# Cross probabilities of layers 2 and 3: transposed by a DMA in two-byte planes, in place of transposes on TensorE

## The chip, the cores and the metric
The kernel runs on one core of one Trainium2 chip. The metric is the device time of one execution in microseconds (us). One execution in addition was taken with the hardware profiler; all rows below come from it. TensorE is PE in the profile (its weight loads PEld), VectorE is DVE, ScalarE is ACT, GpSimd is POOL, and SyncE, which issues all DMAs here, is SP.

## The reference, cut to what matters
Four transformer layers run one after another on `x` (32 batches, 112 tokens, 256 features). All attend to a context `ctx_1024` (32 batches, 375 tokens, 256 features), with 16 heads.

- Layer 0: RMS norm, cross attention with heads of 64 (four shared heads of keys and values), no feed-forward.
- Layer 1: self attention, cross attention with heads of 16, both with 8-bit fake quantisation of queries, keys, values and probabilities, then a gated feed-forward.
- Layer 2: cross attention with 16 heads of 64, all with own keys and values, then a feed-forward with ReLU.
- Layer 3: causal self attention, cross attention with heads of 16, and a feed-forward with ReLU.

The part that matters is the same in all of them:

```python
scores = einsum('bhtd,bhsd->bhts', Q, K) * D ** -0.5
wei = softmax(scores, axis=-1)                 # 112 tokens x 375 context tokens for each head
o = einsum('bhts,bhsd->bhtd', wei, V)
```

The scores come out with the 112 tokens on partitions. The product with V contracts over the 375 context tokens, so the probabilities have to be transposed between the two.

## The kernel before, in words
Batches go in 16 streams of two. Each layer runs over its 16 streams. Activations lie transposed (features on partitions), so that every projection is a few matmuls of 128 x 128 weights against 224 columns (two batches of 112 tokens). All of it is float32 but for layer 1's quantised values, which are bf16.

**Attention.** An *octet* is eight heads of one batch; a *pair* is two heads, four pairs to a cross octet. A *unit* is one head of a cross pair (a unit of self attention holds four heads). For each pair there are these steps, on these engines:

1. `scores` on PE, into one of four PSUM banks, 112 x 375 each. Layers 0, 2 and 3 (`QUADS`) do the scores of two pairs together; they wait for the exps of the pairs before, which free the banks.
2. `max` on DVE (L1595), the negated maximum of each row.
3. `exp` on ACT (L1460), into `e`, which has ES = 8 slots, four pairs' worth, with the sums.
4. `invert` on DVE (L1602), one over the sums.
5. `weigh` on POOL (L1850), each unit's exps times one over its sum, in place, one instruction for each unit.
6. `turn` on PE (`tensor_turn`, L1287): for each unit three transposes of 112 x 125 against the identity, into one of the four `ring` banks of PSUM, and a save by DVE or ACT (L1675, L1500), a copy of 125 x 336 into `probs`. The slots of `e` come free with it.
7. `pv` on PE (L1322 in layer 2, L1329 in layer 3): the product of values and `probs`, an octet at a time. `probs` has two slots, so an octet waits for the product of two octets before.

Layer 1 doesn't turn on PE. DVE writes its 8-bit probabilities as bf16 into `steps` (`eight`, L1637, four slots), and SP issues one transposing DMA for each pair (`flip`, L1878) straight into `probs`. A cross pair of layer 1 has 2 x 3 blocks of 128 columns. Layer 1 therefore cuts the 375 context tokens into 128, 128 and 119 rows, and the other layers into three times 125 (`R`).

**Order.** Each engine's instruction stream is one fixed list that class `Plan` writes at build time. Every step has a place (its pair's index plus an offset) and an assumed cost in microseconds. `arrange` plays the schedule forward with these costs: an engine that is free takes the ready step with the lowest place, and the list that comes out is what the engine executes in order, with semaphore waits for what each step needs. Steps marked "VA" go to DVE or ACT, whichever is free first. PE may run up to `AHEAD = 6` places ahead. "D" is SP's queue: context loads, stream loads, weights, stores and flips, in one order. The costs assumed for a cross pair are among others 1.15 for `weigh`, 0.35 for the PE part of a turn, 0.5 for its save, and 2.5 for a flip of layer 1. A product `pv` is placed at the index of its octet's last pair plus 2.7 (`TURN_LAG` + 0.5), in layer 1 plus 3.4.

In layer 3 a stream has 16 cross pairs and 4 pairs of self attention of the next stream, so 20 pairs; in layer 2 it has 16.

## Time and profile before

| | us |
|---|---|
| median of 3 runs | 4999.22 (4997.36 to 5001.67) |
| the profiled execution, its own time | 5001.85 |
| its span, first to last instruction | 5000.1 |
| PE busy in the span | 4600.5 (92%) |
| DVE, ACT, POOL busy | 2935.6, 2821.5, 2007.6 |

The profile numbers time from the span's start. Layer 0 runs up to about 940, layer 1 to about 2230, layer 2 to about 3840 and layer 3 to the end, with some overlap. "Busy" is the time in which an engine executes something; the granted clock (PEclk) is a share of TensorE's full 2.4 GHz. "Idle before" names what ended an engine's waits. A float32 matmul is in the records as two.

### The profile page before, as it was taken

To read this page: it belongs to the slowest core of one execution; us is meant where nothing else is said; L and a number is where in the kernel's file an instruction comes from. 1 tells how busy PE (TensorE), PEld (TensorE's weight loads), DVE (VectorE), ACT (ScalarE), POOL (GpSimd) and SP (SyncE) were. 2 spreads that over 40 slices of the span, in tenths; PEclk is the share of its full clock that TensorE was granted. 3 is DMA by queue.
4 is the path that set the end of the run, shared out by engine and by line. 5 is a ranking of instruction groups with operands and counts; after the bars stand their busy time and mean duration, and the time that the engine had idled before them with its cause. 6 is when DMAs were issued, how large, how long until landed. Compare 5 with 4: busy or idle time off the path is not lost.

```text
span 5000.1 us, 86857 instructions
## 1 busy us (share of the span) xinstructions
PE 4600.5 (92%) x32032; PEld 3401.8 (68%) x32032; DVE 2935.6 (59%) x6466; ACT 2821.5 (56%) x8969; POOL 2007.6 (40%) x3876
## 2 busy tenths in 40 slices
PE   8999999876877777789999999999999999999998
PEld 5666666655656556567777777777777777777777
DVE  6566556566656665664544454445445766676665
ACT  4555555688888888863333333333334666666664
POOL 3333333466565665642222222222223444444443
PEclk9999999988889888899999999999999999999999
DMA  2000000133333333331000000000000100000000
GB/s 82 21 24 21 25 23 21 51 67 62 64 62 61 62 67 56 68 69 39 11 14 14 14 11 14 14 14 11 14 23 23 37 15 21 21 18 16 20 17 7
DMA packets 279638, 161.54 MB, mean 32 GB/s; under 512 B 244528, under 2 KB 261168, under 8 KB 277808
## 3 DMA queue, kind: packets, MB, share of 16 engines
q1 hardware_dynamic: 279216, 155.99, 12.9%
q8 instruction: 256, 4.19, 0.4%
q14 instruction: 166, 1.36, 0.1%
HBM read 82.53 MB, written 14.68 MB: 19 GB/s over the span
## 4 chain that ended last, share of the span: by engine, by line
PE 83%; ACT 8%; POOL 3%; DVE 2%; issue 2%; DMA 2%; SPq 0%; ACTq 0%; POOLq 0%; DVEq 0%
PE ring L1340 49%; PE ring L1287 11%; PE score L1273 11%; ACT e L1460 5%; PE ring L1322 3%; PE ring L1315 3%; PE ring L1329 2%; DMA probs<-steps 2%; POOL e L1850 1%; PE ring L1284 1%; POOL e L1847 1%; PE ring L1305 1%; ACT work L1521 1%; PE ring L1355 1%; DVE nmax L1595 1%
## 5 line engine op out<-in xcount | busy, mean ns | idle before, releaser
L1850 POOL TENSOR_SCALAR e<-e,rsum 112x375 f32<-112x375 f32 (+1 forms) x2048 | 1067.4, 540 | 2214.8 <-DVE rsum L1602 2178.9
L1500 ACT COPY probs<-ring 125x336 f32<-125x336 f32 (+1 forms) x971 | 400.1, 448 | 1648.2 <-PE ring L1287 1533.9
L1595 DVE TENSOR_REDUCE nmax<-score 112x2 f32<-112x750 f32 (+1 forms) x1152 | 1064.7, 951 | 420.6 <-PE score L1273 420.5
L1460 ACT ACTIVATE e<-score,nmax 112x375 f32<-112x375 f32 (+1 forms) x2048 | 1039.1, 539 | 42.5 <-DVE nmax L1595 38.2
L1340 PE MATMUL ring<-h,weights 128*128 128x224 f32 x3840 | 876.0, 369 | 30.0 <-ACT work L1521 24.9
L1273 PE MATMUL score<-keys,q 64*112 64x375 f32 (+2 forms) x3584 | 608.4, 494 | 232.4 <-ACT e L1460 229.6
L1340 PEld LDWEIGHTS ring<-h,weights 128*128 128x128 f32 x3840 | 724.9, 197 | 104.4 <-ACT work L1521 33.7
L1287 PEld LDWEIGHTS ring<-consts,e 112*125 112x125 f32 x4608 | 584.5, 188 | 230.8 <-issue 178.9
L1287 PE MATMUL ring<-consts,e 112*125 112x112 f32 x4608 | 645.4, 279 | 4.6 <-POOL e L1850 2.6
L1340 PE MATMUL ring<-weights,ctx 128*125 128x512 f32 (+3 forms) x1536 | 588.4, 516 | 0.0
L1273 PEld LDWEIGHTS score<-keys,q 64*112 64x112 f32 (+2 forms) x3584 | 233.0, 166 | 509.2 <-ACT e L1460 287.1
L1460 ACT ACTIVATE e<-score,nmaxc,quant 112x375 f32<-112x375 f32 (+1 forms) x1024 | 555.1, 553 | 10.7
L1340 PE MATMUL ring<-ctx,weights 128*128 128x375 f32 x1536 | 552.4, 485 | 0.2 <-ACT rdev L1509 0.2
L1847 POOL TENSOR_SCALAR e<-e,rsumw 112x375 f32<-112x375 f32 (+1 forms) x1024 | 497.0, 504 | 30.2
L1460 ACT ACTIVATION_READ_ACCUMULATOR e<-score,nmax 112x1 f32 x2048 | 461.7, 225 | 0.0
L1340 PEld LDWEIGHTS ring<-weights,ctx 128*125 128x125 f32 (+2 forms) x1536 | 305.0, 203 | 142.5 <-issue 95.5
L1340 PE MATMUL ring<-work,weights 128*128 128x224 f32 (+1 forms) x1792 | 398.7, 372 | 1.0 <-DVE work L1718 0.6
L1340 PEld LDWEIGHTS ring<-ctx,weights 128*128 128x128 f32 x1536 | 280.5, 191 | 143.2 <-issue 36.5
L1741 DVE COPY values<-ring 125x512 f32<-125x512 f32 (+2 forms) x419 | 196.7, 495 | 302.6 <-PE ring L1340 301.6
L1675 DVE COPY probs<-ring 125x336 f32<-125x336 f32 (+1 forms) x693 | 335.9, 510 | 41.1 <-PE ring L1287 26.6
L1340 PEld LDWEIGHTS ring<-work,weights 128*128 128x128 f32 x1792 | 334.2, 190 | 32.0 <-issue 5.6
L1340 PE MATMUL ring<-heads,weights 128*128 128x224 f32 x1536 | 323.6, 359 | 3.6 <-ACT work L1521 1.8
(123 smaller groups left out, 5104.9 us busy)
## 6 DMA issues: line engine op xcount, KB each, us to landing
ctx<-ctx_t SPq DMA_DIRECT2D x128, 375.0 KB, 3.1
out_t<-x SPq DMA_DIRECT2D x64, 224.0 KB, 1.9
x<-out_t SPq DMA_DIRECT2D x48, 224.0 KB, 2.6
weights<-weights SPq DMA_DIRECT2D x7, 1024.0 KB, 6.2
probs<-steps SPq DMA_TRANSPOSE x320, 2.7
x<-x_t SPq DMA_DIRECT2D x16, 224.0 KB, 2.6
weights<-weights SPq DMA_DIRECT2D x1, 3328.0 KB, 12.3
weights<-weights SPq DMA_DIRECT2D x1, 2304.0 KB, 9.4
```

Of the source, the lines that this page charges most:

```text
L1273: ins = pe.matmul(score_bank(u)[0:S, n * width:(n + 1) * width], lhs, rhs, start=not masked, stop=not masked or n == nt - 1)
L1287: ins = pe.transpose(dst[0:R, c * S:(c + 1) * S], src[:, c * R:(c + 1) * R], idt[0:S, 0:S])
L1315: ins = pe.matmul(ps[64 * odd:64 * odd + 64, 0:4 * S], vs[0:R, c, kv:kv + 64], probs_of(o, c, 4 * odd, 4 * S), start=c == 0, stop=c == last)
L1322: ins = pe.matmul(ps[64 * odd:64 * odd + 64, i * S:(i + 1) * S], vs[0:R, c, hd:hd + 64], probs_of(o, c, 4 * odd + i, S), start=c == 0, sto ...
L1340: ins = pe.matmul(out_, a, b_, start=n == 0, stop=n == len(parts) - 1)
L1460: ins = nc.scalar.activation(e_of(u)[:, n * width:(n + 1) * width], score_bank(u)[0:S, n * width:(n + 1) * width], ACT.Exp, bias=minus, sc ...
L1500: ins = nc.scalar.copy(dst, src)
L1595: ins = dve.tensor_reduce(to, src, AX, ALU.max, negate=True)
L1675: ins = dve.tensor_copy(dst, src)
L1741: ins = dve.tensor_copy(dst, src)
L1847: ins = nc.gpsimd.tensor_scalar(mine, mine, rsumw[0:S, slot(u), n:n + 1], ROUND, ALU.mult, ALU.add)
L1850: ins = nc.gpsimd.tensor_scalar(mine, mine, rsum[0:S, slot(u), n:n + 1], 0.0, ALU.mult, ALU.add)
```

## The change
It concerns the cross attention of layers 2 and 3 (`WORDS`). Step 6 is replaced, the rest stays:

- `split` (POOL): the two-byte halves of the weighed float32 probabilities of a pair are taken apart into two planes in `halves` (three slots): one `tensor_scalar` (times 1, plus 0) on uint16 for each plane, 112 x 750 elements with a stride of two. It frees the slots of `e`.
- `flip` (SP): one transposing DMA for each pair, 112 x 1536 two-byte elements (2 planes x 2 heads x 3 blocks of 128), into `planes` (two slots). It waits for the split and for the merge of two pairs before.
- `merge` (DVE or ACT): one copy for each pair puts the two planes together again as float32 in `probs`, 128 x 1344 two-byte elements.
- The chunks of the context in layers 2 and 3 go from 125, 125, 125 rows to 128, 128, 119.
- `pv` waits for the merges, and is placed at the last pair's index plus 3.9 in layer 2 and 4.3 in layer 3; the last projection of layer 3's cross attention, its norm and the feed-forward are placed 0.7 later.
- `steps` of layer 1 shares the memory of `halves`.

```diff
+WORDS = (2, 3)
+SPLIT_BY = ("G",)
+SPLITS = 3
+PLANES = 2
@@ place_attention
-                if o.layer != 1:
+                if o.layer != 1 and not self.in_words(o):
                     self.turn_of[u] = self.job(p.index + lag + 0.1 * i, "turn", o.layer, o.s, o.b, 0, "VA", u)
...
-                self.pv_of[o] = self.job(p.index + (3.4 if o.layer == 1 else lag + 0.5), "pv", o.layer, o.s, o.b, o.half, PV_BY[o.layer], o)
+                self.pv_of[o] = self.job(p.index + (3.4 if o.layer == 1 else (4.5, 0, 3.9, 4.3)[o.layer] if self.in_words(o) else lag + 0.5), "pv", o.layer, o.s, o.b, o.half, PV_BY[o.layer], o)
+    def in_words(self, o):
+        return o.layer in WORDS and o.attn == "cross"
@@ narrow
+        e += 0.7 if layer == 3 else 0
@@ list_steps
+            if self.in_words(o_):
+                by = SPLIT_BY[self.nth_halved[p] % len(SPLIT_BY)]
+                self.add("split", p, by, 1.7, p.index + 1.4)
+                self.add("flip", p, "D", 4.2, p.index + 1.6)
+                self.add("merge", p, "VA", 1.45, p.index + 2.4)
@@ four_layers
-        steps = sb("steps", [P, STEPSLOTS, 8 * P], BF16)
+        halves = sb("halves", [P, SPLITS, 4 * CHUNKS * P], U16)
+        steps = halves[:, :, :].rearrange("p a n -> p (a n)")[:, 0:STEPSLOTS * 8 * P].bitcast(BF16).rearrange(
+            "p (a n) -> p a n", a=STEPSLOTS)
+        planes = sb("planes", [P, PLANES, 4 * CHUNKS * S], U16)
...
+        def split(eng, wait, p):
+            wait.wait_ge(weighed, nth["weigh", p])
+            for before in plan.halves_before(p):
+                flip_done(wait, before)
+            to = halves_of(p).rearrange("p (h a n) -> p h a n", h=2, a=2)
+            src = e[0:S, pair_slots(p), 0:T].bitcast(U16).rearrange("p a (n h) -> p h a n", h=2)
+            return [(to[:, h, :, 0:T], src[:, h, :, :]) for h in range(2)]
+
+        def merge(wait, p):
+            flip_done(wait, p)
+            wait.done([plan.pv_of[o] for o in plan.probs_before(p.octet)])
+            to = merged_of(p).rearrange("p a n -> p (a n)").bitcast(U16).rearrange("p (m h) -> p m h", h=2)
+            return to, planes_of(p).rearrange("p (h m) -> p m h", h=2)
@@ chunk
-            return (P * c, min(T, P * c + P)) if layer == 1 else (R * c, R * c + R)
+            return (P * c, min(T, P * c + P)) if layer == 1 or layer in WORDS else (R * c, R * c + R)
@@ scalar_program, vector_program
+                    to, src = merge(wait, x_)
+                    nc.scalar.copy(to, src).then_inc(merged["A"], 1)
...
+                    dve.tensor_copy(to, src).then_inc(merged["V"], 1)
@@ scalar_exp
+                elif plan.in_words(before.octet):
+                    wait.wait_ge(halved[plan.split_by[before]], nth["split", before])
@@ pool_program
-            nc.gpsimd.memset(steps[:, :, :], 0.0).then_inc(consts_made, 1)
+            nc.gpsimd.memset(halves[:, :, :], 0).then_inc(consts_made, 1)
+                if kind == "split":
+                    for to, src in split(pool, wait, x_):
+                        ins = nc.gpsimd.tensor_scalar(to, src, 1.0, 0.0, ALU.mult, ALU.add)
+                    ins.then_inc(halved["G"], 1)
+                    continue
@@ sync_program
+                    if plan.in_words(p.octet):
+                        wait.wait_ge(halved[plan.split_by[p]], nth["split", p])
+                        i = plan.nth_halved[p]
+                        if i >= PLANES:
+                            before = plan.halved[i - PLANES]
+                            wait.wait_ge(merged[plan.by[before]], nth["merge", before])
+                        sp.dma_start(planes_of(p).rearrange("p (a n) -> p a n", n=S), halves_of(p),
+                                     transpose=True).then_inc(turned[n % FLIPS], 16)
+                        continue
```

## Rows read from the trace of the kernel before

**Rows 1.** The page's head: span, and each engine's busy time
```profile
span 5000.1 us, 86857 instructions
...
PE 4600.5 (92%) x32032; PEld 3401.8 (68%) x32032; DVE 2935.6 (59%) x6466; ACT 2821.5 (56%) x8969; POOL 2007.6 (40%) x3876
```

**Rows 2.** Busy time by stretch: one stream of layer 2, four of layer 3
```profile
core 0: us, PE busy (x) PEld busy (x) DVE busy (x) ACT busy (x) POOL busy (x), PEclk, DMA share, GB/s
2427.53:2527.80 100.27, 100.27 (x601) 70.95 (x601) 49.08 (x99) 33.52 (x101) 21.12 (x36) 1.00 0.05 13
...
4242.12:4385.11 142.99, 137.22 (x1369) 112.05 (x1369) 98.70 (x239) 90.64 (x339) 66.25 (x140) 0.98 0.07 19
4385.11:4527.90 142.79, 136.64 (x1374) 111.15 (x1373) 99.43 (x241) 91.22 (x343) 66.25 (x140) 0.99 0.06 19
```

**Rows 3.** The chain of waits by line, first stretches of layers 2 and 3
```profile
by line: PE ring L1340 65.9%; PE ring L1287 11.6%; PE score L1273 11.6%; PE ring L1322 9.8%; PE ring L1349 0.8%; PE ring L1355 0.8%
...
by line: PE ring L1340 44.9%; PE ring L1287 15.9%; PE score L1273 10.9%; PE ring L1329 7.3%; PE ring L1284 5.3%; POOL e L1850 3.8%; DVE probs L1675 2.9%; PE ring L1305 2.6%; PE score L1268 2.5%; DVE values L1741 1.2%; issue 0.7%; PE ring L1
```

**Rows 4.** Busy time of L1287's transposes alone, same stretches
```profile
2427.53:2527.80 100.27, 14.37 (x96) 13.21 (x96) 1.00 0.05 13
4242.12:4385.11 142.99, 26.92 (x192) 24.53 (x192) 0.98 0.07 19
```

**Rows 5.** Groups on POOL: layer 3 (3875 to 4875), then 0 to 1000
```profile
L1850 POOL TENSOR_SCALAR e<-e,rsum 112x375 f32<-112x375 f32 x450 | 261.2, 597 | 331.8 <-DVE rsum L1602 299.5 <-PE ring L1340 32.3
...
L1850 POOL TENSOR_SCALAR e<-e,rsum 112x112 f32<-112x112 f32 x448 | 151.2, 365 | 114.8 <-DVE rsum L1602 114.8
...
L1817 POOL TENSOR_TENSOR work<-work 128x375 f32<-128x375 f32 x32 | 34.9, 1091 | 43.7 <-ACT work L1422 43.6
...
L1796 POOL MEMSET steps<- 128x4096 bf16 x1 | 3.5, 3512 | 0.0
```

**Rows 6.** Tile `steps`: layer 1's flips, who waited, time to landing
```profile
L1878 SPq DMA_TRANSPOSE probs<-steps x320: 1202/1209/2266, 930.0 to 2225.3; - x160
...
  PE ring L1305: 27.9, 16
  PE ring L1329: 20.5, 14
...
DMA to landing us min/median/max: 2.6/2.7/11.6
```

**Rows 7.** Timeline of SP's queue: start, length, what
```profile
1228.91 4.07 SPq L1878 DMA_TRANSPOSE probs<-steps  x3
```

**Rows 8.** Busy time and DMA share (column before last) around one flip
```profile
1211.80:1213.20 1.40, 0.41 (x8) 0.28 (x8) 1.40 (x3) 1.37 (x4) 0.20 (x1) 1.00 0.62 123
```

**Rows 9.** Waits of SP's queue over the run: total, times, longest
```profile
SPq L1893 <- PE ring L1340: 1495.2, 72, 50.6
```

**Rows 10.** Groups of copies and the like: layer 3, then whole run
```profile
L1500 ACT COPY probs<-ring 125x336 f32<-125x336 f32 x250 | 100.0, 442 | 230.7 <-PE ring L1287 230.7
L1675 DVE COPY probs<-ring 125x336 f32<-125x336 f32 x200 | 92.8, 499 | 3.8
...
L1595 DVE TENSOR_REDUCE nmax<-score 112x8 f32<-112x896 f32 x56 | 58.5, 1086 | 43.2 <-PE score L1273 43.2
...
L1637 DVE TENSOR_SCALAR steps<-e 112x750 bf16<-112x750 f32 x256 | 146.6, 575 | 74.1 <-POOL e L1847 68.5 <-DMA probs<-steps 5.0
...
L1417 ACT ACTIVATE squares<-h 128x448 f32<-128x448 f32 x128 | 72.5, 600 | 13.6 <-DVE h L1680 13.6
...
L1433 ACT ACTIVATE heads<-heads 128x1792 f32<-128x1792 f32 x16 | 27.2, 1697 | 0.2
```

**Rows 11.** Timeline of layer 3, from scores to their weighing
```profile
4303.04 0.90 PE L1273 MATMUL score<-keys,q 32*112 32x375 f32 x8
...
4307.88 2.30 POOL L1850 TENSOR_SCALAR e<-e,rsum 112x375 f32<-112x375 f32 x4 [4.02 <-DVE rsum L1602]
```

**Rows 12.** Busy time by stretch, layer 1
```profile
1125.00:1250.00 125.00, 86.01 (x572) 64.25 (x573) 77.39 (x172) 106.20 (x336) 81.06 (x170) 0.81 0.30 62
```

98 lines of the change are left out of this document (81 added, 17 removed).

## The prediction
> **What bounds the kernel now.** I read the page's head first. In a span of 5000.1 us TensorE (PE) is busy 92% and nothing else above 59% [rows 1]; but the stages differ, so the chain of waits comes next, since it repeats. In layer 2 one stream of two batches takes 100.27 us, in layer 3 two streams take 142.99 us, 71.5 each, and the next two 142.79; I use 71.4 a stream. The windows over exactly these stretches [rows 2] show PE busy for all 100.27 us in layer 2, with DVE at 49.1, ACT 33.5 and POOL 21.1. In layer 3 PE is busy 137.2 of 143.0, DVE 98.7, ACT 90.6, POOL 66.3, so 33.1 us of POOL a stream. The chain by line [rows 3] says what of PE sets the pace: the turns of the cross probabilities (L1287) are 11.6% of the chain in layer 2 and 15.9% in layer 3. Nothing else there is touched by the change, except that layer 3's chain also holds 3.8% of waits on POOL's weighing and 2.9% on DVE's copies of turned probabilities.
>
> **Step 1, PE's turns go.** 11.6% of 100.27 is 11.6 us for 96 transposes, so 0.121 us each; 15.9% of 142.99 is 22.7 us for 192, 0.118 each. I don't use their busy time (14.37 and 26.92 us [rows 4]), which counts the overlap with the neighbours. Sixteen streams a layer: 16 x 11.6 = 186 us in layer 2 and 16 x 11.4 = 182 us in layer 3, 368 us in all, if PE stays the bound. The matmuls that read the result keep their number and width; only the rows of a chunk go from 125, 125, 125 to 128, 128, 119. I cost that at nothing: it is the same moving columns on the same engine.
>
> **Step 2, POOL's split comes.** Two instructions a pair, each 112 x 750 two-byte elements. No row has POOL reading 16-bit data. Weighing takes 261.2/450 = 0.580 us for 375 elements and 151.2/448 = 0.338 for 112 [rows 5], so 0.92 ns an element over 0.234 fixed; 750 elements are 0.93 us, a pair 1.85 us. The low bound is the two-byte memset, 3.512/4096 = 0.857 ns an element, so 0.64 us, 1.29 a pair (it reads nothing). Above, plain proportion to the 375 row is 1.16, 2.32 a pair. Far above is the two-input add, 1.09 us for 375, 4.4 a pair. I take 1.85: one input and a scalar operation is what weighing is, and the memset shows that two-byte elements are not dear to write. The plan's own entry, 1.7, lies beside it, and its entry for weighing (1.15) beside 2 x 0.58.
> The Trainium skill, GPSIMD Engine Reference, Performance versus the Vector engine, gives about 1.8 cycles an element at 1.2 GHz as the best one-input rate. By it a split is an estimated 2.25 us a pair and POOL 69.1 us a stream in layer 3, for a total of an estimated 4840 us, where the rows give 4733. The rows' slope of 0.92 ns is below that rate of 1.5 ns, and the rows decide.
>
> Sixteen cross pairs a stream make 29.6 us more of POOL. Layer 2: 21.1 + 29.6 = 50.7 against PE's 100.27 - 11.6 = 88.7. PE stays the bound, and 186 us come off. Layer 3: 33.1 + 29.6 = 62.7, against 71.4 - 11.4 = 60.0 of PE. The bound passes to POOL.
>
> **Step 3, the flip.** It replaces nothing on PE's path, it adds latency. Layer 1's cross flips carry 6 runs of 128 columns; the new ones 12. One flip now takes SP 1.209 us to issue, lands after 2.7, three go out in 4.07 us, and one fills the 16 DMA engines for 0.62 x 1.40 = 0.87 us [rows 6 to 8]. Twice the runs: issue 2.4, engines 1.7, landing between 2.4 + 1.5 = 3.9 (the rest is fixed) and 5.4 (all doubles). I take 4.4. Pairs come every 88.7/16 = 5.5 us in layer 2 and 66/16 = 4.1 in layer 3, so neither queue nor engines fill. With two plane slots a flip waits for the merge two pairs back: 4.4 + 1.5 every two pairs, against 8.2. Behind a waiting flip in SP's order stand the context loads, the stream loads and stores. Context loads sit in SP waiting on PE for 1495 us over the run [rows 9]: a load for two batches ahead as soon as its slot is free; it lands in a few us and is wanted a batch (some 33 us) later, so some us of delay are hidden. With that cover gone, one would cost its lateness on PE.
>
> **Step 4, the merge.** 1344 two-byte elements on DVE or ACT, in place of two copies of 336 from PSUM (ACT 0.40 us each, DVE 0.46 [rows 10]). ACT takes 0.60 for 448 and 1.70 for 1792 elements, so 1.33 for 1344. DVE has two ends: its PSUM max, 1.086 for 896, is 1.63 in proportion; SBUF to SBUF it wrote 750 two-byte steps in 0.575, which is 1.03 [rows 10]. I take 1.6, the slow end, because the source here is strided and the steps' is not. Half on each engine in layer 3: DVE 49.4 - 6.6 + 8 x 1.6 = 55.6 us a stream, ACT 45.3 - 7.1 + 8 x 1.33 = 48.8. Both stay under 62.7, so this is off the path. But the merge waits for a flip, and behind it on ACT and DVE stand exps and maxima, and behind those the next scores. What hides that is only the plan's placing.
>
> **Step 5, latency to the product.** In layer 3 scores that start at 4303.04 are weighed by 4310.18, 7.1 us [rows 11]; split, flip and merge add 1.85 + 4.4 + 1.5 = 7.8, so 14.9. The plan puts the product 4.3 pairs (of 20 a stream, 3.3 us each) behind the last pair, 17.5 us behind the scores of its quad. The margin is 2.6 us, and POOL would be 95% busy, with a self pair's weighing of 2.7 us in its queue. So PE will wait at some products. In layer 2, 3.9 pairs of 5.5 us are ample.
>
> How near does a bound engine come to full here? PE reaches 100% in layer 2 and 96% in layer 3 [rows 2]; in layer 1 ACT, the busiest, reaches only 106.2 of 125 us, 85%, with PE's clock at 0.81 [rows 12]. Weighing isn't inside the loop of scores, maxima and exps as ACT is, since four pairs of slots lie between. I take 95%: 62.7/0.95 = 66.0 us a stream, so layer 3 gives 16 x 5.4 = 86 us and not 182.
>
> **Small terms.** The end of the kernel: after the last pair nothing covers split, flip and merge, 7.8 us, and two turns with their copies (about 1.5) go: +6. The products, the norm and the feed-forward behind them don't change. The first memset grows by 0.4 us.
>
> **Sum.** 5000.1 - 186 - 86 + 6 = 4734 of span. The execution took 5001.85, 1.75 more than its span, and the runs' median is 4999.22, 2.6 below it: 4734 + 1.75 - 2.6 = 4733.
>
> **Rivals.**
> A, *PE stays the bound in layer 3 too* (split near its low bound, 1.3 to 1.5, so POOL at 54 to 57). Then 5000 - 186 - 182 + 6 - 1 = 4637. For it: POOL's weighing is fast and the plan assumes 1.7. Against: it needs PE to wait as little as now, with POOL nearly as full as PE.
> B, *layer 3 gains nothing*. Either the split costs the proportional 2.32 a pair, POOL 70.2, at 95% 73.9 us; or it costs 1.85 and POOL reaches only layer 1's 85%, 73.8 us. Both are 2.4 us a stream worse than 71.4, 39 us: 5000 - 186 + 39 + 6 - 1 = 4858.
> C, *the flips set the pace* (the other side). If a flip holds the transposing path for twice today's whole latency, 5.4 us, one behind another, layer 3 takes 16 x 5.4 = 86.4 us a stream: +15.0 x 16 = 240; layer 2's 88.7 just covers it. 5000 - 186 + 240 + 5 = 5059. It decides from (71.4 + 11.6)/16 = 5.2 us a flip. Against it: three flips issued in 4.07 us and 0.87 us of engine time for one. For it: PE waited 48 us for flips in layer 1, where they are half as long [rows 6].
> The Trainium skill, VectorE: DVE Perf Modes, The three transpose paths, sides with C: it puts a 128 x 128 bf16 transpose at 390 ns on TensorE and 1309 ns by DMA, and advises TensorE where PSUM will do. By it, twelve tiles one after another would be an estimated 15.7 us a pair, 251 us a stream in both layers and some 10,300 us in all; this trace, with six tiles landed in 2.7 us, doesn't agree.
> D, *a split of over 2.8 us a pair*, towards the two-input row: POOL (33.1 + 16 x 2.8)/0.95 = 82 us eats the gain of layer 2; at 4.4 it would be 109 us, some 5420 in all.
>
> **Chances.** Forecast 0.58, A 0.18, B 0.15, C 0.05, D 0.04. A measurement of this kernel tells 0.2% (10 us) from no change. C and D make slower 0.08; between B and C lies a mix that ends at no change, 0.02; faster 0.90. The likeliest case alone spans 4665 to 4810 (POOL at 98% with the plan's 1.7, to 90% with 2.0). The range takes in A and B: 4630 to 4870; outside stay C, D and a little of A's edge.
>
> **What would show it.** Right: no L1287-like transposes of 112 x 125 past layer 1; layer 2's stream at 88 to 90 us with PE full; layer 3's POOL over 90% busy at about 66 us a stream, its split instructions at 0.93 us; flips landing at about 4.4; merges 1.3 to 1.6. Step 2 is wrong if the split isn't within 0.65 to 1.16 us; step 5 if POOL sits idle in layer 3 while PE waits for merges; C if flips land later than 5.2 us as a rule. PE's clock in layer 3, now 0.98, should fall somewhat if PE waits; were it to fall to layer 1's 0.81 with POOL not full, PE would be the bound by its clock and B the outcome.

## The result, and the profile after

The changed kernel takes 4943.27 us (median of 4 runs, 4941.93 to 4946.87) against 4998.55 (4 runs): a ratio of 0.989, interval 0.9872 to 0.9907. That is 55 us faster, where 265 were forecast. The profiled execution took 4946.87 us. One of the four executions of `all_small_self` below, the profiled one, took 5782 us at a granted clock of 0.73 and is left out of its median.

The page's head, which answers to [rows 1]:

```profile
span 4945.1 us, 83152 instructions
...
PE 4355.7 (88%) x28960; PEld 3088.0 (62%) x28960; DVE 2949.4 (60%) x6068; ACT 2953.4 (60%) x8855; POOL 2967.2 (60%) x4900
```

PE lost 245 us of busy time and the span only 55; POOL gained 960. The stages part. First the windows: one stream of layer 2, then twice two streams of layer 3 (columns as in [rows 2]).

```profile
core 0: us, PE busy (x) PEld busy (x) DVE busy (x) ACT busy (x) POOL busy (x), PEclk, DMA share, GB/s
2701.71:2792.07 90.36, 90.36 (x505) 60.23 (x505) 47.47 (x88) 38.08 (x95) 48.91 (x68) 1.00 0.38 76
3974.05:4127.41 153.36, 125.22 (x1178) 92.72 (x1177) 105.57 (x213) 97.63 (x330) 131.63 (x204) 0.92 0.46 89
4127.41:4279.56 152.15, 125.62 (x1177) 92.92 (x1177) 103.17 (x213) 97.21 (x330) 132.21 (x204) 0.91 0.48 90
```

Layer 2: 90.36 us a stream, PE still full, beside 100.27: 9.9 x 16 = 158 us came off. Layer 3: 76.7 and 76.1 us a stream beside 71.4. Over the four, 305.5 us, it is 76.4: 5.0 x 16 = 79 us were lost. PE is 82% busy there, POOL 86%, and PE's granted clock fell from 0.98 to 0.92 and 0.91. 158 - 79 is 79, and the rest of the way down to 55 lies at layer 3's start and end. The starts of the norms' squares (ACT, L1417 before, L1516 now) show it: the changed kernel is 155.4 us ahead at 3842.00 (now 3686.58), 140.9 at 3910.34, 79.1 at 4835.49 (now 4756.44), and 55.0 at the end. So thirteen steady streams lose 62 us, the stretch before them 14.5 and the last one 24.0.

The chain by line, layer 2 (four streams from 2701.71), then layer 3 (four from 3974.05), beside [rows 3]:

```profile
by line: PE ring L1438 74.1%; PE score L1367 12.8%; PE ring L1419 10.9%; PE ring L1447 1.3%; PE ring L1453 0.8%
...
by line: POOL e L1965 18.3%; POOL halves L1947 17.9%; PE ring L1438 16.1%; DMA planes<-halves 9.9%; issue 9.1%; PE score L1367 3.7%; DVE nmax L1699 3.0%; PE ring L1427 2.5%; PE ring L1378 2.4%; DVE probs L1735 2.2%; ACT e L1564 1.9%; POOL s
```

In layer 2 only PE is left. In layer 3 the chain runs over every engine: weighing (L1965), splitting (L1947), projections (L1438), flips, and "issue". No line holds a fifth.

The new steps, as groups in layer 3 (3900 to 4900), then in layer 2 (2500 to 3800). Columns: operation and shapes, count, busy us, mean ns, idle before.

```profile
L1947 POOL TENSOR_SCALAR halves<-e 112x750 uint16<-112x750 uint16 x432 | 391.9, 927 | 9.0 <-DMA planes<-halves 0.3
L1965 POOL TENSOR_SCALAR e<-e,rsum 112x375 f32<-112x375 f32 x432 | 279.7, 660 | 48.5 <-DVE rsum L1706 48.1
L1735 DVE COPY probs<-planes 128x1344 uint16<-128x1344 uint16 x140 | 142.8, 1020 | 55.5 <-DMA planes<-halves 54.3 <-PE ring L1427 0.8
L1538 ACT COPY probs<-planes 128x1344 uint16<-128x1344 uint16 x75 | 109.7, 1462 | 54.8 <-DMA planes<-halves 54.3
...
L1947 POOL TENSOR_SCALAR halves<-e 112x750 uint16<-112x750 uint16 x452 | 369.4, 835 | 15.2
```

A split takes 0.93 us in layer 3 and 0.84 in layer 2; 0.93 was forecast. A weighing took 597 ns on the mean before in layer 3 [rows 5] and takes 660 now. A merge is 1.02 us on DVE (1.6 forecast) and 1.46 on ACT (1.33).

The tile `planes` over the run, beside [rows 6]: the flips' issue and landing, the merges, and who waited.

```profile
L1997 SPq DMA_TRANSPOSE planes<-halves x512: 1259/1363/5316, 2229.9 to 4907.3; - x171
L1735 DVE COPY probs<-planes x315: 809/852/2047, 2233.7 to 4910.8; 128x1344 uint16<-128x1344 uint16 x158
...
  ACT probs L1538: 158.7, 88
  DVE probs L1735: 82.3, 92
  PE ring L1427: 47.1, 19
...
DMA to landing us min/median/max: 3.4/3.5/9.6
```

A flip takes SP 1.36 us and lands after 3.5, below the low end of Step 3 (3.9). But DVE and ACT stand 241 us in their queues for flips, 113 of them in layer 2 (by `l2_only` below), where PE is full all the same. And PE's products of layer 3 (L1427) wait 47.1 us in 19 waits for merged probabilities, 2.9 us a stream.

**One round of layer 3.** A round is the scores of two pairs, their maxima, their exps, and the next scores, whose PSUM banks those exps free. Timeline of the changed kernel (start, length, engine, line, operation, count, idle before):

```profile
3997.78 0.90 PE L1367 MATMUL score<-keys,q 32*112 32x375 f32 x8
...
3999.34 1.62 POOL L1947 TENSOR_SCALAR halves<-e 112x750 uint16<-112x750 uint16 x2
4000.32 1.35 DVE L1735 COPY probs<-planes 128x1344 uint16<-128x1344 uint16 x1 [1.75 <-DMA planes<-halves]
4000.93 1.25 POOL L1922 TENSOR_TENSOR squares<-squares 128x224 f32<-128x224 f32 x1
4001.60 1.77 DVE L1699 TENSOR_REDUCE nmax<-score 112x2 f32<-112x750 f32 x2
4002.33 1.09 PE L1453 MATMUL ring<-squares,mean_w 128*128 128x224 f32 x2 [3.65 <-POOL squares L1922]
4002.73 0.57 ACT L1564 ACTIVATE e<-score,nmax 112x375 f32<-112x375 f32 x1
...
4005.16 0.56 ACT L1564 ACTIVATE e<-score,nmax 112x375 f32<-112x375 f32 x1
...
4005.87 0.98 PE L1367 MATMUL score<-keys,q 32*112 32x375 f32 x4 [2.45 <-ACT e L1564]
```

The scores are ready at 3998.68. DVE, in its fixed order, has the merge (L1735) next, stands 1.75 us for its flip, merges, and only then takes the maxima, at 4001.60. On POOL the norm's add (L1922) comes behind two splits (L1947), so PE waits 3.65 us for it. The next scores start 8.09 us after these. PE had nothing from 3999 to 4002.3, and its granted clock went down behind that, as windows over these stretches show (the column before the last two):

```profile
3997.00:3999.00 2.00, 1.45 (x10) 0.58 (x10) 0.68 (x2) 0.39 (x1) 2.00 (x5) 1.00 1.60 120
3999.00:4002.00 3.00, 0.00 (x0) 0.00 (x0) 1.68 (x2) 0.82 (x2) 3.00 (x4) 0.68 0.65 145
4002.00:4006.00 4.00, 1.22 (x6) 0.64 (x6) 2.79 (x6) 3.85 (x12) 3.91 (x7) 0.50 0.73 124
4006.00:4010.00 4.00, 4.00 (x15) 2.71 (x16) 3.01 (x5) 3.19 (x7) 3.91 (x5) 0.50 0.47 89
```

At 0.50 (1.2 GHz) two records of a norm's matmul take 1.09 us (L1453 above) beside 0.62 at 1.00 (L1447, of the same shape, at 3997.24). From windows of 1 us each I summed PE's busy time times (1 - clock), the share of its busy time that full clock would have saved: 5.1 us over the 286 us of [rows 2]'s four streams (1.3 a stream), and 18.7 over the four streams after (4.7).

What PE itself waits for over these four streams (from 3974.05), in us in total, times, longest:

```profile
PE score L1362 <- ACT e L1564: 13.8, 6, 4.3
PE score L1367 <- ACT e L1564: 12.4, 8, 3.4
PE ring L1453 <- POOL squares L1922: 9.4, 4, 3.6
```

Of the 54.7 us in which PE is idle there, 26.2 are scores waiting for exps, 10.9 a norm's squares on POOL (1.5 of them for L1917) and 8.4 merges. Before, over four streams, scores waited 5.1 us for exps.

### The profile page after: what moved, and what is told of

It reads as the page before. It is cut to its first block, busy times and chain, and to the rows that moved or that the text cites. A ratio compares the mean times of both kernels' runs of the same rounds, so it can differ in the third digit from the quotient of the medians.

```text
span 4945.1 us, 83152 instructions
## 1 busy us (share of the span) xinstructions
PE 4355.7 (88%) x28960; PEld 3088.0 (62%) x28960; DVE 2949.4 (60%) x6068; ACT 2953.4 (60%) x8855; POOL 2967.2 (60%) x4900
## 4 chain that ended last, share of the span: by engine, by line
PE 68%; POOL 11%; ACT 8%; DVE 4%; issue 4%; DMA 4%; SPq 0%; ACTq 0%; POOLq 0%; DVEq 0%
PE ring L1438 45%; PE score L1367 9%; ACT e L1564 5%; POOL e L1965 4%; POOL halves L1947 4%; PE ring L1381 3%; PE ring L1419 3%; PE ring L1412 3%; DMA probs<-halves 2%; DMA planes<-halves 2%; DVE nmax L1699 1%; PE ring L1427 1%; POOL e L1962 1%; ACT work L1625 1%; PE ring L1378 1%
## 5 line engine op out<-in xcount | busy, mean ns | idle before, releaser
L1965 POOL TENSOR_SCALAR e<-e,rsum 112x375 f32<-112x375 f32 (+1 forms) x2048 | 1140.2, 571 | 1167.3 <-DVE rsum L1706 1162.0
L1438 PE MATMUL ring<-h,weights 128*128 128x224 f32 x3840 | 891.3, 375 | 55.0 <-ACT h L1527 27.0
L1947 POOL TENSOR_SCALAR halves<-e 112x750 uint16<-112x750 uint16 x1024 | 877.3, 876 | 28.4 <-DMA planes<-halves 0.3
L1438 PEld LDWEIGHTS ring<-h,weights 128*128 128x128 f32 x3840 | 747.7, 201 | 182.0 <-issue 89.6
L1438 PE MATMUL ring<-weights,ctx 128*128 128x256 f32 (+3 forms) x1536 | 589.9, 517 | 0.0
L1438 PE MATMUL ring<-ctx,weights 128*128 128x375 f32 x1536 | 572.5, 495 | 1.0 <-DVE heads L1800 0.8
L1438 PEld LDWEIGHTS ring<-weights,ctx 128*128 128x128 f32 (+1 forms) x1536 | 307.5, 203 | 153.4 <-issue 98.9
L1604 ACT COPY probs<-ring 125x336 f32<-125x336 f32 (+1 forms) x350 | 144.0, 460 | 433.3 <-PE ring L1381 368.8
L1438 PEld LDWEIGHTS ring<-ctx,weights 128*128 128x128 f32 x1536 | 282.2, 192 | 188.5 <-issue 81.8
L1438 PE MATMUL ring<-work,weights 128*128 128x224 f32 (+1 forms) x1792 | 398.8, 373 | 1.0 <-DVE work L1828 0.6
L1538 ACT COPY probs<-planes 128x1344 uint16<-128x1344 uint16 x197 | 287.8, 1462 | 159.8 <-DMA planes<-halves 158.7
L1438 PEld LDWEIGHTS ring<-work,weights 128*128 128x128 f32 x1792 | 334.0, 190 | 41.3 <-issue 13.2
L1735 DVE COPY probs<-planes 128x1344 uint16<-128x1344 uint16 x315 | 303.1, 962 | 86.5 <-DMA planes<-halves 82.3
L1851 DVE COPY values<-ring 128x512 f32<-128x512 f32 (+5 forms) x353 | 186.6, 547 | 277.4 <-PE ring L1438 276.4
L1438 PE MATMUL ring<-heads,weights 128*128 128x224 f32 x1536 | 327.2, 363 | 6.0 <-DVE heads L1806 2.1
```

The source lines that it names most:

```text
L1438: ins = pe.matmul(out_, a, b_, start=n == 0, stop=n == len(parts) - 1)
L1538: nc.scalar.copy(to, src).then_inc(merged["A"], 1)
L1735: dve.tensor_copy(to, src).then_inc(merged["V"], 1)
L1851: ins = dve.tensor_copy(dst, src)
L1947: ins = nc.gpsimd.tensor_scalar(to, src, 1.0, 0.0, ALU.mult, ALU.add)
L1965: ins = nc.gpsimd.tensor_scalar(mine, mine, rsum[0:S, slot(u), n:n + 1], 0.0, ALU.mult, ALU.add)
```

## The experiments

Eighteen kernels were run. Unless said otherwise each is the changed kernel with the edit shown, compared with the kernel before on the same chip.

### Which layer gains, and is it POOL's load

`l2_only` is layer 2 alone in the new form. `l3_half` gives layer 3's new form to every second batch; the turns of the others are placed 3.4 pairs behind, not 2.2, and each waits for the product that frees its slot. `one_plane` leaves the second plane's split out in layer 3 (its output isn't the reference's).

```diff
l2_only
-WORDS = (2, 3)
+WORDS = (2,)
l3_half
+        return (o.layer == 2 or o.layer == 3 and o.b % 2 == 0) and o.attn == "cross"
+            lag = 3.4 if o.layer == 3 and o.attn == "cross" else TURN_LAG
...
one_plane
-            return [(to[:, h, :, 0:T], src[:, h, :, :]) for h in range(2)]
+            return [(to[:, h, :, 0:T], src[:, h, :, :]) for h in range(1 if p.octet.layer == 3 else 2)]
```

> The split, flip and merge in layer 2 alone; layer 3 turns on PE as in the kernel before. Theory (layer 2 gains 9.9 us a stream, layer 3 loses 4.9 us a stream): layer 2 at 90.4 us a stream, layer 3 back at 71.4, total 4998 - 158 = 4840 us. Rival (layer 3 only looks slower because the transition and the end moved, and its own change costs nothing): the total stays near the changed kernel's 4943 us.

> Layer 2 wholly by the DMA, in layer 3 only the even batches, the odd ones turned on PE (their turns placed 3.4 pairs behind instead of 2.2, and never ahead of the product that frees their slot). Theory POOL (POOL's work sets layer 3's pace): POOL falls from 66 to about 33 + 8 x 1.7 = 47 us a stream, PE carries 71.4 - 5 = 66, the stream takes 67 to 68 us and the total is 4770 to 4790 us. Theory latency (the wait for split, flip and merge sets it, whatever POOL has to do): half the streams' octets still wait, layer 3 at 72 to 76 us a stream, total 4850 to 4915 us.

> Leaves out the split of the second plane in layer 3 (the low halves of the probabilities are split, the high halves are not, so the numbers are not those of the reference); flips and merges stay whole. POOL has 13 us less a stream there. Theory POOL: the stream falls from 76.3 to 65 to 69 us, total 4770 to 4830 us. Theory latency: each split is 0.8 us shorter out of some 8 us behind the weighing, the stream stays at 75 to 76 us and the total above 4920 us.

| | us | ratio | interval | layer 3, us a stream | POOL busy there |
|---|---|---|---|---|---|
| `l2_only` | 4840.9 | 0.9681 | 0.9667 to 0.9696 | 70.6 | 47% |
| `l3_half` | 4913.66 | 0.9826 | 0.9812 to 0.9841 | 75.0 | 64% |
| `one_plane` | 4907.89 | 0.9813 | 0.9799 to 0.9828 | 73.6 | 71% |

`l2_only` gains 158 us, what layer 2's streams showed, and is 102 us faster than the changed kernel. The theory that POOL's load alone bounds layer 3 fell: with POOL at 64% and 71% a stream still takes 75.0 and 73.6 us, more than the 70.6 with all turns on PE. The load isn't free either: `one_plane`, at 4908, lies between what either theory foretold, and the split that it leaves out is worth 35 us.

### Where the merges stand

```diff
-                self.add("merge", p, "VA", 1.45, p.index + 2.4)
+                self.add("merge", p, "A", 1.45, p.index + 2.4)
```

> All merges on ACT instead of DVE or ACT. Theory contention (DVE's merges, 0.85 us for 1344 elements, hold POOL up while they run): weighing in layer 2 falls back from 0.62 to 0.58 us, splits in layer 3 from 0.91 to 0.82 us, no split above 1 us. POOL gets 6 us a stream back in layer 3, ACT goes to 62 us a stream: 72 to 75 us a stream, total 4870 to 4930 us, unless ACT at over 80% busy holds up the exps. Rival (POOL's long instructions come from its own queue or from other DVE work): weighing stays at 0.62 and splits of over 1 us remain; total 4940 to 4990 us, as ACT carries more.

5008.77 us, 1.0016 (1.0006 to 1.0025). Groups of layer 3 (3950 to 4950) with all merges on ACT:

```profile
L1947 POOL TENSOR_SCALAR halves<-e 112x750 uint16<-112x750 uint16 x398 | 339.1, 874 | 6.3 <-DMA planes<-halves 0.3
L1538 ACT COPY probs<-planes 128x1344 uint16<-128x1344 uint16 x201 | 292.4, 1478 | 68.9 <-DMA planes<-halves 68.4 <-PE ring L1427 0.2
L1965 POOL TENSOR_SCALAR e<-e,rsum 112x375 f32<-112x375 f32 x398 | 233.9, 600 | 72.4 <-DVE rsum L1706 72.4
```

With no merge on DVE, POOL's weighing goes from 660 ns to 600 and its split from 927 to 874. So DVE's merges held POOL up. The changed kernel's records say it too (layer 3, 3900 to 4800): the 84 splits that overlap a DVE merge for over three tenths of their length take 1.21 us on the mean, the 289 that meet none 0.85. Thirty-two of each a stream make that 32 x (0.060 + 0.053) = 3.6 us of POOL. The Trainium skill, GPSIMD Engine Reference, Specifications, says that GpSimd shares its SBUF interfaces with VectorE and contends with VectorE instructions that run in a two-port mode or have two inputs in SBUF. A merge has one input and no trace shows its mode; that it slows POOL agrees. Yet the kernel is 65 us slower, 81.8 us a stream. The tile `planes` shows where: PE's products wait 129.9 us for merges, not 47.1. In layer 3 (4000 to 4300) that is 7.6 us a stream beside 2.1 in the changed kernel, while scores wait for exps 5.5 us a stream beside 6.6. So merges that queue up on ACT delay the products, and not the exps in the first place. That POOL's relief is worth less than this speaks against POOL as the bound too.

### Each new step made small

In layer 3 alone, the split is cut to 2 x 32 elements in one instruction, the flip to one run of 128 columns, the merge to 84 of its 1344 elements. The output isn't the reference's.

```diff
flip_small
+                        runs = 1 if p.octet.layer == 3 else 4 * CHUNKS
+                        sp.dma_start(planes_of(p).rearrange("p (a n) -> p a n", n=S)[:, 0:runs, :],
+                                     halves_of(p)[:, 0:runs * P], transpose=True).then_inc(turned[n % FLIPS], 16)
merge_small
+            if p.octet.layer == 3:
+                return to[:, 0:84, :], src[:, 0:84, :]
all_small: both of these, and
+            if p.octet.layer == 3:
+                return [(to[:, 0, :, 0:32], src[:, 0, :, 0:32])]
```

> In layer 3 alone the flip transposes one run of 128 columns instead of 12; split and merge stay whole, so the probabilities are not the reference's. Theory latency: flips land about 1.3 us earlier and leave the DMA engines free, merges and products wait less, the stream falls from 76.3 to 72 to 74 us, total 4870 to 4910 us. Rival load on the engines: the stream stays at 75.5 to 76.3, total 4930 to 4943 us.

> In layer 3 alone the merge copies 84 of 1344 elements, so the probabilities are not the reference's; split and flip stay whole. Theory load on DVE and ACT (the merges stand ahead of maxima and exps and hold the scores up, and DVE's hold POOL up): some 17 us of the two engines' time and 5 to 6 of POOL's go a stream, the stream falls from 76.3 to 69 to 72 us, total 4825 to 4875 us. Rival POOL or latency: POOL still has 60 us and the flip its 3.5, the stream stays at 74 to 76, total 4905 to 4940 us.

> In layer 3 alone the split does one instruction of 2 x 32 elements, the flip one run of 128 columns, the merge the first sixteenth part of the octet pair (84 of 1344 elements); the probabilities there are therefore not the reference's. All instructions, waits and places stay but for the second split. Theory load (POOL, flip and merge work make layer 3 slow): the stream falls from 76.3 to PE's 60 to 64 us, total 4680 to 4750 us. Rival order (the plan's placing and the chain of waits set it, whatever each step takes): over 70 us a stream, total above 4840 us.

| | us | ratio | interval | less than the changed kernel |
|---|---|---|---|---|
| `flip_small` | 4929.4 | 0.9859 | 0.9844 to 0.9875 | 14 |
| `merge_small` | 4884.37 | 0.9768 | 0.9753 to 0.9782 | 59 |
| `one_plane` (above) | 4907.89 | 0.9813 | 0.9799 to 0.9828 | 35 |
| `all_small` | 4834.84 | 0.9673 | 0.9657 to 0.9689 | 108 |

The parts are 0.9 us a stream for the flips' size, 3.7 for the merges, 2.2 for half the splits. All together are 6.8, which is what layer 3 lost (5.0) and 2 us more.

What a merge costs is mostly not its wait for a flip. In `merge_small` DVE and ACT still stand 241.5 us for flips, as in the changed kernel (241.0), and 59 us come off. In `flip_small`, where a flip of layer 3 lands after 2.3 us and not 3.6, they stand 160.2 us, and only 14 come off. So it is the merges' own time on DVE and ACT, ahead of maxima and exps, and what they take from POOL, whose split falls from 931 to 861 ns with them short (3900 to 4600).

`all_small` is the sharpest reading of the study. It has PE's turns gone (11.4 us a stream by Step 1) and little work in their place; the waits, the written order and a flip's landing of 2.3 us stay. A stream takes 69.3 us, only 1.3 less than `l2_only`'s 70.6, where the turns are there; the two totals are 6 us apart, at the edge of the noise. Windows over the quarters of one stream, columns as above, first of `l2_only`:

```profile
4015.72:4033.38 17.66, 17.66 (x138) 15.26 (x137) 12.10 (x28) 9.38 (x42) 7.86 (x21) 1.00 0.00 1
4033.38:4051.04 17.66, 17.66 (x196) 14.65 (x196) 12.47 (x32) 11.52 (x36) 8.63 (x15) 1.00 0.09 28
4051.04:4068.70 17.66, 16.55 (x162) 13.03 (x160) 12.07 (x33) 12.04 (x53) 6.04 (x12) 1.00 0.08 23
4068.70:4086.36 17.66, 15.67 (x194) 11.79 (x195) 12.24 (x30) 13.27 (x47) 10.45 (x24) 1.00 0.09 24
```

The same of `all_small`:

```profile
3943.72:3961.05 17.33, 17.33 (x128) 14.60 (x128) 10.43 (x26) 8.94 (x36) 9.82 (x25) 1.00 0.11 31
3961.05:3978.38 17.33, 12.47 (x99) 8.10 (x99) 10.39 (x27) 9.28 (x31) 8.91 (x19) 0.81 0.13 34
3978.38:3995.71 17.33, 12.34 (x166) 8.12 (x164) 8.59 (x22) 10.21 (x50) 8.04 (x19) 1.00 0.04 8
3995.71:4013.04 17.33, 15.12 (x150) 11.22 (x154) 14.22 (x36) 13.32 (x52) 12.57 (x27) 1.00 0.12 32
```

The same of the changed kernel:

```profile
3974.05:3993.14 19.09, 19.09 (x141) 15.61 (x141) 13.17 (x31) 11.29 (x42) 14.92 (x30) 1.00 0.34 75
3993.14:4012.23 19.09, 12.26 (x110) 7.83 (x112) 12.89 (x24) 11.74 (x32) 17.52 (x22) 0.73 0.67 114
4012.23:4031.32 19.09, 13.96 (x162) 10.23 (x151) 11.25 (x20) 10.94 (x50) 17.14 (x24) 0.82 0.47 91
4031.32:4050.41 19.09, 16.40 (x188) 12.47 (x188) 16.08 (x37) 16.54 (x61) 18.73 (x31) 1.00 0.35 75
```

All three begin with a quarter in which PE is full. With turns PE is full in the second too and 89% to 94% busy in the rest. Without them it is 71% to 87% busy there in `all_small` and 64% to 86% in the changed kernel. In the changed kernel the same quarters hold POOL at 90% to 98%, and the clock falls to 0.73 and 0.82. In `l2_only` 11.7 of the stream's 13.3 us of turns (L1381) lie in those last three quarters, and in `all_small` PE idles 12.1 us there. So the turns in layer 3 lay to a large part where PE, in this order, has nothing else to do.

The round at the same place in `all_small`, from its timeline, shows what is left without the new steps' work:

```profile
3966.61 0.90 PE L1372 MATMUL score<-keys,q 32*112 32x375 f32 x8
3968.88 1.78 DVE L1704 TENSOR_REDUCE nmax<-score 112x2 f32<-112x750 f32 x2
...
3969.85 0.57 ACT L1569 ACTIVATE e<-score,nmax 112x375 f32<-112x375 f32 x1 [0.57 <-DVE nmax L1704]
...
3972.98 1.61 PE L1372 MATMUL score<-keys,q 32*112 32x375 f32 x8 [3.47 <-ACT e L1569]
```

6.37 us from scores to scores, against 8.09; PE still waits 3.47 us for the exps, since its list has no projection ready while the norm is being made. Over the four streams from 3943.72 scores wait for exps 23.3 us, where PE idles 38.3:

```profile
PE score L1372 <- ACT e L1569: 12.6, 8, 3.5
PE score L1367 <- ACT e L1569: 10.7, 6, 2.0
```

### What holds the rest: maxima, pairs, self attention, the order, the reach

All of these but `l2_only_max`, `pairs` and `l3_small_self_turn` build on `all_small`. The short maximum is over 94 of a head's 375 scores, so 188 of a pair's 750 (the text below says 94): 0.35 us, not 0.93. `self` makes one head's exp in four of layer 3's self attention (work left out in both). `all_small_plan` also places layer 3's product 3.4 pairs behind, not 4.3, and `AHEAD` holds for all layers. `pairs` makes layer 3's scores pair by pair and keeps the output.

```diff
all_small_max, l2_only_max
+                    few = 94 if o.layer == 3 and not is_own(o) else nt * width
+                    src = score[0:S, first:first + 2, 0:few].rearrange("p a (i n) -> p a i n", i=nt)
all_small_pairs, pairs
+QUADS = (0, 2)
all_small_self, l3_small_self_turn (this one with WORDS = (2,))
+                for n in range(1 if o.layer == 3 else count_of(o)):
all_small_plan
+... (4.5, 0, 3.9, 3.4)[o.layer] ...
+                self.add("split", p, by, 0.25 if few else 1.7, p.index + 1.4)
+                self.add("flip", p, "D", 2.0 if few else 4.2, p.index + 1.6)
+                self.add("merge", p, "VA", 0.3 if few else 1.45, p.index + 2.4)
all_small_ahead
+AHEAD = 10.0
```

> As all_small (split, flip and merge of layer 3 nearly empty; the probabilities not the reference's), and in layer 3's cross attention the maximum is taken over 94 of a pair's 750 scores, so DVE's maxima there take some 0.3 us instead of 0.93. Theory loop (layer 3 is bound by the round of scores, maximum, exps and the next scores, which the four score banks allow only one of at a time): each of 8 quads a stream loses 0.6 us of that round, the stream falls from 69.3 to 63 to 65 us, total from 4835 to 4750 to 4785. Rival (PE or the plan's order of products sets it): under 1.5 us a stream, total 4810 to 4835 us.

> As l2_only, with the same short maximum in layer 3's cross attention. There layer 3 turns on PE, which is busy 96% of the stream's 70.7 us. Theory: the loop is just covered by PE, so the shorter maximum takes away only the gaps: 0.5 to 2 us a stream, total 4810 to 4835 us. Rival (DVE's load sets layer 3 in both): as much as in all_small_max, 4 to 6 us a stream, total 4745 to 4775.

> As all_small, with layer 3's scores done a pair at a time instead of two pairs (layer 3 taken out of QUADS): scores of a pair wait only for the exps of two pairs before, so that PE, DVE and ACT overlap in the round, for about 0.8 us more of PE for each two pairs. Theory loop: the stream falls from 69.3 to 64 to 67 us although PE has 6 to 8 us more to do, total 4750 to 4800 us. Rival order: PE's added work shows, the stream goes to 72 or more, total above 4880 us.

> The changed kernel whole, with layer 3's scores a pair at a time. Theory (two bounds lie close together in layer 3: the loop at 69 us and POOL, 60 us of its own work and 6 of contention, behind it): the loop's bound goes, POOL's stays, 70 to 74 us a stream, total 4850 to 4905 us, still not under l2_only's 4841. Rival: no better than the changed kernel's 4943 us, or worse by PE's added work, up to 5040.

> Layer 3's split is one short instruction of 2 x 32 elements, its flip one run of 128, its merge 84 of 1344 elements (as before in this study), and of layer 3's self attention only one head's exp in four is made. All of these leave work out. The run without the last edit took 4834.8 us, 69.3 us a stream of layer 3, and a stream there shows PE full in its first quarter and 64 to 84% busy in the other three. Theory (a stream of layer 3 has a stretch of projections in which PE is full, and stretches of self pairs, maxima and exps in which ACT and DVE set the pace, so that the removed turns only filled idle PE there): with 16.2 us of ACT a stream taken out of the self pairs (12 exps of 112 columns and more for each pair, at 0.34 us each), the other three quarters shorten: a stream of 62 to 66 us, 4720 to 4785 in all. Rival (the written order of PE holds these stretches, whoever is free): not below 4815. The same edit where PE has the turns too and is 96% busy is the run sent beside it.

> Layer 2 in the new form, layer 3 with its turns on PE, as in the run that took 4840.9 us; of layer 3's self attention only one head's exp in four is made (work left out). Theory (PE's own work bounds layer 3 when it has the turns: 96% busy at 70.7 us): at most what PE idles there, 2 us a stream, comes off: 4808 to 4841. Rival (the exps of the self pairs hold layer 3 in both forms alike): it falls by as much as the run beside it does, 50 to 110 us, to 4730 to 4790.

> The small split, flip and merge of layer 3 again (work left out; 4834.8 us without this edit), and the order is written with costs that fit them: 0.25 for the split, 2.0 for the flip, 0.3 for the merge, and the product 3.4 pairs behind, not 4.3. Rival to the stretch theory (the order, written for costs that these steps don't have, is what keeps the almost free steps at 69.3 us a stream): PE near full at 60 to 64 us a stream, 4690 to 4750. Theory (the self pairs' and the round's own work holds it): within 15 us of 4834.8.

> The small split, flip and merge of layer 3 again (work left out; 4834.8 us without this edit), and PE may run 10 places ahead in the written order, not 6. Theory (PE idles in the stretches of self pairs for want of work that is ready): more of the projections may be drawn into them, 4800 to 4830. Rival (nothing more is ready, or the order isn't what holds it): within 10 us of 4834.8. A second rival: work drawn ahead delays scores that ACT waits for, 4845 to 4880.

| | us | ratio | interval | beside |
|---|---|---|---|---|
| `all_small_max` | 4812.14 | 0.9624 | 0.9608 to 0.964 | 4834.84: -23 |
| `l2_only_max` | 4838.27 | 0.9677 | 0.9663 to 0.9691 | 4840.9: -3 |
| `all_small_pairs` | 4863.74 | 0.9728 | 0.9714 to 0.9743 | 4834.84: +29 |
| `pairs` | 4971.68 | 0.9946 | 0.9931 to 0.9961 | 4943.27: +28 |
| `all_small_self` | 4823.5 | 0.9647 | 0.9631 to 0.9663 | 4834.84: -11 |
| `l3_small_self_turn` | 4845.62 | 0.9693 | 0.9678 to 0.9707 | 4840.9: +5 |
| `all_small_plan` | 4857.91 | 0.9719 | 0.9704 to 0.9733 | 4834.84: +23 |
| `all_small_ahead` | 4904.75 | 0.981 | 0.9794 to 0.9827 | 4834.84: +70 |

With the turns on PE, neither maxima nor self exps matter (-3 and +5 us are within the intervals): PE is the bound. Without them, a much shorter maximum gives 1.4 us a stream, where my theory of the round foretold over four, and leaving out 24 of a stream's 32 exps of self attention gives 0.7. Scores pair by pair, foretold as a gain, are a loss in both forms. My theory that the exps of the self pairs pace the starved quarters foretold 50 to 110 us for the latter and fell. Costs that fit the small steps, and a longer reach for PE, make it slower: 71.1 and 71.7 us a stream of layer 3, and the rest of the 70 us of `all_small_ahead` lies outside layer 3's steady streams. Neither run rules the written order out. In `all_small_plan` PE waits 53.3 us for merges (18.9 in `all_small`), since the product was moved nearer as well, so costs and place weren't tried apart. That two edits of the order alone move the time by 23 and 70 us says that it matters; a better order stays an untested rival. No single work step among these is the pacer of a stream without turns.

### Feeding PE in its idle time

The output is kept. Throwaway matmuls of 128 x 128 fill places in layer 3 where PE idles: two ahead of each quad's scores, in the banks that its first exps have freed, six ahead of a norm's second matmul, and in `fill` four more ahead of a product. At 1.85 ns a column one is 0.24 us.

```diff
+                wait.wait_ge(expd, nth["exp", plan.pairs[p.index - 2]])
+                fill(pe, score_bank(p.units[0]), 2)
...
+                if j.layer == 3 and j.kind in FILLED:
+                    fill(pe, ps, FILLED[j.kind])
+FILLED = {"var": 6}                # fill_light
+FILLED = {"var": 6, "pv": 4}       # fill
```

> The changed kernel, whose output is kept, with throwaway matmuls of 128 x 128 on PE in layer 3 where its trace shows PE idle: two before the scores of two pairs, behind the wait for the first pair's exps and ahead of that for the second's, and six ahead of each second matmul of a norm, in a ring bank that the real matmul then overwrites. At 1.85 ns a column (eight records of 256 columns in 1.89 us) one is 0.24 us, so 9.1 us a stream. In the changed kernel PE has the lower clock for 51 of 306 us in layer 3, always after a stretch without matmuls, and does 18.7 us of its busy time there for nothing, 4.7 us a stream, beside 1.3 with the turns. Clock theory (part of what layer 3 lost is the clock that PE keeps only while it is fed, and the turns fed it): these matmuls lie mostly in idle time, the clock share of layer 3 rises from 0.92 to 0.96 or more, and the kernel is faster, 4890 to 4935. Rival (the clock's fall is only a mark of the waits, and costs nothing since the waits are for other engines): not faster, 4940 to 5010, as the uncovered ones add up.

> As the run beside it, with four more such matmuls ahead of each product with the values in layer 3: 14 us a stream in all, where PE idles 13.7. Clock theory: the clock is at 0.98 or more in layer 3; the time lies between a gain like that of the run beside it and a loss of what is uncovered, 4880 to 4960. Rival: above the run beside it and above the changed kernel, 4960 to 5060.

| | us | ratio | interval | us at half clock in 300 of layer 3 | PE time lost to it, a stream |
|---|---|---|---|---|---|
| changed kernel | 4943.27 | 0.989 | 0.9872 to 0.9907 | 51 | 4.7 |
| `fill_light` | 4989.64 | 0.9981 | 0.9972 to 0.999 | 20 | 2.3 |
| `fill` | 5037.38 | 1.0076 | 1.0063 to 1.009 | 14 | 1.7 |

The last two columns are worked out from windows of 1 us. Two streams of `fill_light`, as a window:

```profile
4140.08:4298.63 158.55, 138.69 (x1329) 109.00 (x1329) 103.39 (x213) 97.95 (x330) 130.21 (x204) 0.97 0.47 86
```

And of `fill`:

```profile
4144.62:4308.86 164.24, 150.20 (x1426) 121.66 (x1425) 104.22 (x214) 98.12 (x330) 128.53 (x204) 0.97 0.44 84
```

The clock comes back (0.92 to 0.97), and the kernel is slower, as the rival had it: the 9.1 and some 15 us of fillers (38 and 62 a stream) lengthen a stream from 76.4 to 79.3 and 82.1 us, though 2.4 and 3.0 us of PE's time come back. Probably they delay scores that the other engines wait for; the runs don't show it. Keeping PE warm this way doesn't pay. What the clock costs by itself these runs can't say, since every filler also takes PE's time.

### Layer 0 in place of layer 3

```diff
+        return (o.layer == 2 or o.layer == 0 and o.s < STREAMS - 1) and o.attn == "cross"
...
```

> Split, flip and merge in layer 2 and in layer 0 (its first 15 streams), layer 3 as before the change; layer 1's first four slots of steps get their padding cleared. A layer 0 stream takes about 58.5 us, PE full, and would need 48.6 of PE, about 51 of POOL (21.6 + 16 x 1.63 + contention), DVE about 42, ACT 40. Theory load: POOL nearly full but no self attention beside it, 52 to 54 us a stream, total 4840 - 15 x 5.5 = 4760 us (4740 to 4790). Rival (a stage with pairs every 3.3 us is too short for the longer chain, as in layer 3): no gain or a loss in layer 0, total 4840 to 4910 us.

4925.47 us, 0.9853 (0.9838 to 0.9867), output kept: 85 us slower than `l2_only`. Layer 0's 57.7 us a stream, PE 99% busy before, becomes 60.3 on the mean (59.0 in its second half) with POOL at 88% to 91%. But that is the smaller part. In the profiled executions the norm at 859.85 us in `l2_only` comes 28 us later here (887.88), and the one at 2103.80 comes 89 later (2192.96). So 61 us are lost in layer 1, whose steps are the same but for some clearing at its start. Its written order came out otherwise: this run has 60 matmul records of L1438 in a row (12.38 us) where `l2_only` has 32 (6.46). I haven't tried whether that order is the cause.

In these three stages the change paid only where pairs come slowly (5.6 us apart in layer 2, 3.8 in layers 3 and 0).

## Why the prediction was wrong

The forecast of 4733 was 210 us too low; 4943 lies outside the range. Layer 2 is 28 of them, layer 3's steady rate is 86 + 79 = 165, and the rest lies at layer 3's start and end, where 24 us beyond that rate were lost and +6 was forecast.

- **Step 1, layer 2: right in kind, the term too large.** PE stays full and the stream is bound by it. A turn's transpose was worth 9.9/96 = 0.103 us, not 0.121. Its share of the chain (11.6%) seems to include overlap with the neighbours: the projections are 74.1% of 90.36 = 67.0 us of the chain now, 65.9% of 100.27 = 66.1 before [rows 3]. `l2_only` confirms 158 us.
- **Step 1, layer 3: this step failed.** It took 11.4 us a stream as PE's saving, so that PE's 60.0 stood as a floor close to reach. `all_small`, with the turns gone and little work for them, reaches 69.3. PE 96% busy [rows 2] did not mean that its work was all on the path: taken away, part of it left idle time in the same place. The chain showed the turns at 15.9% since PE was doing them; it doesn't tell what PE would have waited for without them. The waits do: scores for exps, 1.3 us a stream before, 5.8 in `all_small`.
- **Step 2: the split's size right, the conclusion wrong.** 0.93 us in layer 3 as forecast, and POOL's 65.8 us a stream beside 62.7; the missing 3 us are weighings (128 of the cross pairs took 83.6 us over four streams, 74.2 before, and 128 of the self pairs 46.8, 43.2 before). But the bound did not pass to POOL: `one_plane` (POOL 71%) and `l3_half` (64%) stay at 73.6 and 75.0 us. The Trainium skill, GPSIMD Engine Reference, Performance versus the Vector engine, gives 1.8 cycles an element at 1.2 GHz as the best case, an estimated 1.1 us for 750; the median split takes 0.83, so the measurement decides against it here.
- **Step 3: better than forecast.** Landing 3.5 us, issue 1.36 (2.4 forecast), and the flips' size is worth 0.9 us a stream. Rival C fell. By the Trainium skill, VectorE: DVE Perf Modes, The three transpose paths, a flip would be an estimated 15.7 us; the trace doesn't agree.
- **Step 4: "off the path" failed.** DVE's merge is cheaper than forecast (1.02 us) and yet the merges are the dearest of the three: 3.7 us a stream (`merge_small`). The text named what stands behind them, exps and maxima, and priced it at nothing because the plan's placing hides it. The round above shows it unhidden: a merge waits 1.75 us for its flip in DVE's queue and takes 1.35, with maxima ready behind it. The waits for flips are the smaller part of the price, as `merge_small` and `flip_small` show. What merges take from POOL has no term in the text at all.
- **Step 5: right that PE waits at products, wrong in how near POOL comes to full.** The products' waits are 2.9 us a stream. POOL is 86% busy, not 95%, and idle while PE waits for merges, the text's own sign that this step is wrong. A stream got slower (76.4), not faster (66.0). That is rival B's second form, "POOL reaches only layer 1's 85%", which gave 73.8 us; with the measured 65.8 us of work it would be 77.4, near the 76.4 found. The number fits by luck and the cause doesn't, as `one_plane` shows: it has 71% of 73.6, 52 us of POOL a stream, which at 85% would be 62 us, and takes 73.6.
- **The likeliest span** was mis-summed at its upper end: POOL at 90% with 2.0 a pair is 65.1/0.90 = 72.3 us a stream, 4834 in all, not 4810. It changes neither the range nor the outcome.
- **The clock** was named as a sign (0.98 to fall somewhat), with no price. It is 0.92, and PE loses 4.7 us of busy time a stream to it, 3.4 more than before.

Shown: layer 2's gain and its size; that the work of layer 3's new steps costs some 7 us a stream, more than half of it the merges; that without it the turns' removal is worth about 1 us a stream there, in this order and with the new waits kept; that POOL's load alone doesn't bound it; that DVE's merges slow POOL; that half of PE's idle time in layer 3 is scores waiting for exps. Argued from the timelines only: that the round of scores, maxima and exps, crossing with the norm, is what makes these waits. Open: whether another written order would let the saving appear, or which part of that round would have to go, and what the clock costs by itself. A product placed later than 4.3 pairs, merges on DVE alone, and one plane of the split on DVE were not tried.

## The best version

`l2_only`: 4840.9 us, 0.9681 of the kernel before and 102 us under the changed kernel, with the output kept.

## What to carry to other kernels

An engine that is 96% busy may hold work that others' latency leaves room for. Before counting a removed operation at its chain share, ask in which stretches of the stream it lies and what would end PE's wait there next; a run with the operation gone and as little as possible in its place gives the ceiling for the order at hand, and here it would have shown about 1 us a stream instead of 11. Price a cheap step in an in-order queue by the work that stands behind it and by the engines that it slows, and take its parts away one at a time: here shortening the merges gave 59 us and shortening the flips that they wait for 14. And apply such an exchange stage by stage: it paid only in the stage whose pairs come slowest.
